# Attention stage of a fused layer: local result from masked scores as weights, values streamed

## The reference, cut to what matters

```python
def step(carry, xs):
    S, z = carry
    qc, kc, vcc = xs
    scores = jnp.einsum('bhid,bhjd->bhij', qc, kc) * mask
    num = jnp.einsum('bhij,bhje->bhie', scores, vcc) + jnp.einsum('bhid,bhde->bhie', qc, S)
    den = scores.sum(-1) + jnp.einsum('bhid,bhd->bhi', qc, z)
    out = num / jnp.clip(den, EPS)[..., None]
    S = S + jnp.einsum('bhjd,bhje->bhde', kc, vcc)
    z = z + kc.sum(2)
    return ((S, z), out)
```

```python
gprob = jax.nn.sigmoid(jax.nn.relu(coarse_repr @ eg_w1.T + eg_b1) @ eg_w2.T + eg_b2)
...
output = gate * memory_output + (1.0 - gate) * local_output
output = output.transpose(0, 2, 1, 3).reshape(B, S, H)
return output @ w_o.T
```

## Time and profile before

| what | us |
|---|---|
| median of 3 runs (679.31 to 690.9) | 687.66 |
| profiled execution | 685.47 |
| its span, first to last instruction | 683.6 |
| TensorE products busy | 601.4 |
| VectorE busy | 490.6 |
| ScalarE busy | 342.1 |
| GpSimd busy | 287.2 |

### The profile page before, as it was taken

One profiled execution on the slowest core, in us unless ns is written; L12 is line 12 of the kernel. 1 busy time (PEld: TensorE's weight loads), 2 busy tenths in 40 slices (PEclk: granted clock), 3 DMA queues, 4 the chain that ended last, 5 costly groups with the idle time before them and its releaser, 6 DMA issues. The chain is left out here.

```text
span 683.6 us, 23842 instructions
## 1 busy us (share of the span) xinstructions
PE 601.4 (88%) x8665; PEld 500.9 (73%) x8665; DVE 490.6 (72%) x1461; ACT 342.1 (50%) x870; POOL 287.2 (42%) x375
## 2 busy tenths in 40 slices
PE   1999998998995999999999588988989899889995
PEld 0787786887875899999999476766766676667773
DVE  3484565465575677777777566888888888878896
ACT  4538548548544444444444334555555555555542
POOL 2055064074072830000000303567666766666664
PEclk9999999999998899999999756999999999999997
DMA  9025535446156344445554502432443244323120
GB/s 306 34 106 200 198 138 204 164 152 217 74 199 234 113 129 154 152 150 152 156 164 128 156 23 67 131 95 66 144 142 95 66 157 130 95 66 95 34 66 32
DMA packets 62230, 88.60 MB, mean 130 GB/s; under 512 B 8532, under 2 KB 48436, under 8 KB 62132
## 3 DMA queue, kind: packets, MB, share of 16 engines
q1 hardware_dynamic: 52340, 66.61, 29.3%
q0 software_dynamic: 7520, 20.07, 9.3%
q10 hardware_dynamic: 2272, 0.53, 0.4%
HBM read 46.94 MB, written 40.24 MB: 128 GB/s over the span
## 5 line engine op out<-in xcount | busy, mean ns | idle before, releaser
L1703 POOL DMA_INDIRECT yg<-d_grouped_y,from_row x64 | 63.7, 996 | 15.5 <-issue 11.6
L986 ACT ACTIVATE silu<-e_up 128x176 f32<-128x176 f32 x72 | 22.9, 318 | 91.0 <-PE e_up L91 91.0
L89 PE MATMUL e_up<-wb,xb 128*128 x144 | 51.0, 354 | 1.5 <-DVE xb L1009 1.5
L1639 DVE TENSOR_TENSOR probs<-a_ring,causal_s 128x256 f32<-128x256 f32 x128 | 45.2, 414 | 9.3 <-PE a_ring L1400 8.9
L1545 ACT ACTIVATE hid<-a_ring,b 64x128 f32<-64x128 f32 x32 | 11.6, 363 | 79.0 <-PE a_ring L1428 75.8
L1528 ACT ACTIVATE with_mem<-a_ring 128x340 f32<-128x340 f32 x128 | 46.8, 447 | 4.5 <-PE a_ring L1381 4.5
L91 PE MATMUL e_up<-wb,xb 128*128 x144 | 46.9, 326 | 0.0
L90 PE MATMUL e_up<-wb,xb 128*128 x144 | 46.8, 325 | 0.0
L833 POOL TENSOR_TENSOR ticks<-lane 128x1 f32<-128x1 f32 x4 | 2.2, 561 | 97.7 <-DVE slot_i L746 97.7
L1418 PE MATMUL a_ring<-wo,attT 128*128 128x256 f32 x128 | 37.3, 416 | 6.5 <-ACT attT L1537 3.2
L1023 DVE TENSOR_TENSOR h_sb<-e_up,silu 128x128 f32<-128x128 f32 x72 | 21.0, 292 | 29.8 <-ACT silu L986 23.0
(11 more groups left out here) (290 smaller groups left out, 2064.6 us busy)
## 6 DMA issues: line engine op xcount, KB each, us to landing
v<-d_rows SPq DMA_DIRECT2D x77, 128.0 KB, 2.0
d_grouped_y<-y_sb SPq DMA_DIRECT2D x73, 128.0 KB, 1.9
d_v<-v_half SPq DMA_DIRECT2D x8, 544.0 KB
d_q<-halves SPq DMA_DIRECT2D x8, 512.0 KB
d_k<-halves SPq DMA_DIRECT2D x8, 512.0 KB
total<-d_base SPq DMA_DIRECT2D x8, 512.0 KB
out<-total SPq DMA_DIRECT2D x7, 512.0 KB, 3.9
v<-d_v SPq DMA_DIRECT2D x6, 544.0 KB
```

Source lines behind the costliest of these rows:

```text
L89: pe.matmul(out, a[0], b[0], start=start, stop=False)
L1639: dve.tensor_tensor(probs[:, j, :, :], ps[:, 0:4 * CH].rearrange("p (h i) -> p h i", i=CH), causal[:, :].unsqueeze(1).broadcast_to([P, 4, ...
L1703: pool.indirect_dma_start(yg[tile % GATHERS][:, k, :], None, d["grouped_y"], bass.IndirectOffsetOnAxis(ap=c["from"][:, k, tile:tile + 1], ...
```

## The change

The `values` step goes, and with it its two banks, ScalarE's two copies and the buffer `valT`. In `local` the masked scores `probs` (64 x 64 for a head and half) become the weights and the 17 columns of `v` stream; the result comes out with tokens on the partitions, in the bank and place where the state products already are, and is added to them. Half 0 uses partitions 0 to 63 of both memories, half 1 uses 64 to 127. The ring has 15 uses a tile, and the bank of `local` now follows that of `oproj` by seven. In the list, `state` with j = 1 moves in front of `gate`. VectorE's masking waits for `local` of the tile before, where it waited for its `values`.

```diff
-        order += [("values", b, t, 0), ("values", b, t, 1), ("gate", b, t, 0)]
         if t < NT - 1:
             order.append(("state", b, t, 1))
+        order.append(("gate", b, t, 0))
...
-                    elif what == "values":
-
-                        to = [ps, use_bank(pe, (what, b, n, 1))]
-                        for n_done, g in enumerate((0, 2, 1, 3)):
-                            if n_done % 2 == 0:
-                                since(pe, s_probs, b * NT * 4 + t * 4 + n_done + 2)
-                            for h in range(2):
-                                of = slice(h * CH, (h + 1) * CH)
-                                for i in range(4):
-                                    m, pair, r = g // 2, 2 * (g % 2) + i // 2, i % 2
-                                    mm = pe.matmul(to[h][VC * i:VC * i + HE, g * CH:(g + 1) * CH], v_of[of, b % 2, t, 4 * g + i, :],
-                                                   probs[of, pair, 2 * m + r, :], start=True, stop=True)
-                                if g == 3:
-                                    mm.then_inc(ready["values"], 1)
-                        continue
...
-                        since(pe, s_valT, b * 2 * NT + 2 * (t + 1))
-                        for g in range(4):
-                            mm = pe.matmul(ps[:, g * P:(g + 1) * P], valT[:, g, :], c["ident"][:, :],
-                                           start=(t == 0 and g == 0), stop=True, is_transpose=True,
-                                           skip_group_check=(t > 0 or g > 0))
+                        since(pe, s_probs, b * NT * 4 + t * 4 + 4)
+                        for n_done in range(NH):
+                            m, pair, r = n_done // HH, n_done % HH // 2, n_done % 2
+                            for h in range(2):
+                                of = slice(h * CH, (h + 1) * CH)
+                                mm = pe.matmul(ps[of, n_done * VC:n_done * VC + HE], probs[of, pair, 2 * m + r, :],
+                                               v_of[of, b % 2, t, n_done, :],
+                                               start=(t == 0 and n_done == 0), stop=True,
+                                               skip_group_check=(t > 0 or n_done > 0))
...
-                    elif what == "values":
-                        since(act, ready["local"], b * NT + t)
-                        act.activation(valT[:, :, j * CH:(j + 1) * CH], ps[:, 0:4 * CH].rearrange("p (g n) -> p g n", g=4),
-                                       ACT.Copy).then_inc(s_valT, 1)
...
-                        since(dve, ready["values"], b * 2 * NT + 2 * t)
+                        since(dve, ready["local"], b * NT + t)
```

More of the change, by code:

```diff
@@ L1190, in attention_phase @@
         ones = c["before"]
-        valT = sb("valT", [P, 4, P])
         with_mem = [sb(f"with_mem{q}", [P, NP, WN + NR2]) for q in range(3)]
@@ L1252, in attention_phase @@
                  ("mean", "norms", "keys", "scores", "outT", "coarseT",
-                  "hidden", "values", "local", "gate", "state", "oproj")}
-        s_valT = sem("a_valT")
+                  "hidden", "local", "gate", "state", "oproj")}
         s_mask = sem("a_mask")
@@ L1267, in attention_phase @@
             "mean": 1, "norms": NB3 * NT, "keys": NT, "scores": 4 * NT, "outT": NT, "coarseT": NT, "hidden": NT,
-            "values": 2 * NT, "local": NT, "gate": NT, "state": STATES, "oproj": NT}
+            "local": NT, "gate": NT, "state": STATES, "oproj": NT}
         last_reader = {
@@ L1272, in attention_phase @@
             "keys": s_ktok, "scores": s_probs, "outT": s_attT, "coarseT": s_coarseT, "hidden": s_hid,
-            "values": s_valT, "local": s_local, "gate": s_e, "oproj": s_sum}
+            "local": s_local, "gate": s_e, "oproj": s_sum}
         def nth(name, n, j):
-            return {"scores": 4 * n + j, "norms": NB3 * n + j, "values": 2 * n + j}.get(name, n) + 1
+            return {"scores": 4 * n + j, "norms": NB3 * n + j}.get(name, n) + 1
         def read_count(b, name, n, j):
@@ L1361, in walk @@
                     tok = slice(t * P, (t + 1) * P)
-                    if what in ("scores", "norms", "values") and j:
+                    if what in ("scores", "norms") and j:
                         continue
@@ L1507, in walk @@
                         continue
-                    if what not in ("keys", "outT", "coarseT", "hidden", "values", "gate",
+                    if what not in ("keys", "outT", "coarseT", "hidden", "gate",
                                     "mexp", "norms", "rows"):
```

## The result

The changed kernel takes 702.7 us as the median of four runs (698.87 to 709.37). The kernel before, run beside it, takes 684.6 (679.31 to 690.9). The ratio is 1.0253, with an interval from 1.0188 to 1.0318: slower, most likely by over 2%. The ratio is of the fast executions alone; 709.37 was a slow one. Forecast was 685, with no change.

The account below looks back on a forecast made before the run. A loop over GpSimd's sum and gathers was taken to bind each attention tile. From 685.47 us profiled, -3 and +1.5 gave 684.0, or 686.2 with the median's offset; 685 was forecast, 8 in 10 for 670 to 708.

Parts of the forecast that it names:

- likeliest case: Attention stage: the loop over GpSimd still binds, so time stays within 678 to 694 us; chance 0.62.
- Steady cost: 0: Attention tiles at full clock: scores start 0.25 us late, VectorE's later waits take it up, so nothing is lost.
- The cover: VectorE's waits of 0.46 to 0.97 us a tile absorb late scores, until new products exceed about 2.2 to 2.7 us.
- at full clock but for the first 20 us: TensorE's clock in the attention stage, about 404 to 672 us, as read from the profile before the change.
- The price of the new products: TensorE's 64 local products a tile: 1.73 us, with two quadrants loading at once, 54 ns each load.
- the slow rival: All 64 weight loads of the local products go one after another, 3.46 us a tile, about 720 us; chance 0.14.
- The loop over GpSimd: Sum and gathers 6.33 us, 0.48 to the fold, fold and products 1.64, 0.08 onward: 8.53 us sets the tile.
- The first two tiles: Attention's start at about half clock: new products 3.46 us against 2.76 removed, 0.7 a tile, +1.5 us for both.
- The rows' wait: GpSimd waits 5.5 us in 14 tiles for ScalarE's scaled rows behind the copies; 3 us counted as gain.
- The moved state update: Second state update ahead of gate waits for the first fold; local results still arrive in time, so cost 0.
- rival for faster: TensorE and ScalarE bind the attention tile, so stops and the rows' wait go: 17 us, about 669; chance 0.17.

Follow-up runs that it names:

- e1_stream64: Changed kernel with each new local product streaming 64 columns of values instead of 17, same loads: 685.5 us, ratio 1.0016 to the kernel before.
- e6_keep_clock: Changed kernel with 32 columns streamed and one extra 256-column product a tile before each second state update: 704.2 us, median of four.

## Why the prediction was wrong

The forecast was no change; measured was a loss of 18 us, inside the range (up to 708) and outside the likeliest case's own (678 to 694). The step that failed is "Steady cost: 0. The cover ends when the new products take over about 2.2 to 2.7 us", and under it the premise "at full clock but for the first 20 us", read from the earlier trace rows and carried over to the changed kernel without a word.

- *The clock, left out.* It was counted for the first two tiles alone. But the change takes away the 64 streams of 64 columns that line 1440 had, and puts loads of 64 columns with streams of 17 in their place. After that the granted clock falls again and again. Shown by e1_stream64: the same loads in the same order with 64 columns streamed, and clock and time are back. The 16.1 us between the two profiled executions (700.6 and 684.5) go with the clock: 53 us more at 1.2 GHz after 424, and 16 more before (0.39 x 20 / 0.5), so 0.23 us of time for each us at the lower clock. The two parts differ: 6.5 of the 16.1 us are there at the first output projection (424.7 against 418.3), 0.4 for each us, and 9.6 come after it, 0.18 for each. A path that ran through TensorE alone would lose half a us for each. That it is less after 424 fits the slack of the loop, which pays a part.
- *The price of the new products.* Estimated 1.73 us by loads at 54 ns for a pair of quadrants, measured 1.97, so 62 ns a pair. The two quadrants do load at once (two loads one after the other would be 108), and the slow rival (3.46) is out. The Trainium skill ("TensorE: Matmul & The Clock Gate", Part 3), by which a load overlaps a running product only in other row groups, gave 2.2; the measurement lies between the two. With 64 columns streamed, and the prediction's 0.84 ns a column for the stream too, an estimate by that rule is 54 + 54 a pair, 3.46 us, where that run has its scores 2.01 us after its first local product; there the trace does not agree.
- *The loop over GpSimd.* Right as the limit of the kernel before, and of the changed one as long as the clock is up: e1_stream64 shows the loop as nearly its whole chain in the attention stage, the two runs with plain loads show the gathers as the cause of the late signal. But the loop binds by little: without the gathers the kernel before gains 1.2% (0.4 to 2.0), and its tiles at full clock go from 8.43 to 8.22 us, not to 7.5.
- *How deep the cover is.* The prediction read it from VectorE's waits (0.46 to 0.97 us). TensorE's own length of a tile, 7.89 us at full clock, against the 8.53 of the loop leaves 0.64, which fits the chain of e6_keep_clock. At full clock the forecast's step holds, then: 1.97 us is under its 2.2 to 2.7. A fall of the clock for 3.4 us costs TensorE 1.25 us and more: it goes through the cover in the tile in which it comes.
- *The first two tiles.* Counted 1.5 us. The output projection of the first tile starts 2.4 us later (424.7 against 422.3). With 64 columns it starts at 418.3: the clock rises earlier there than in either kernel.
- *The rows' wait.* Right as a wait (5.5 to 0.7 us), and worth nothing.
- *The moved state update.* Costed at 0, measured 0 in both directions.

That the loop over TensorE and ScalarE binds (669) was a rival for faster. TensorE did come to bind, but with a longer path.

Why e1_stream64 takes 8.41 us a tile (first to last start of the output projection, 418.3 to 678.9, over 31) and the kernel before 8.28 (422.3 to 678.9) was not followed further. The 4 us are made up for by the earlier rise of the clock; so a few us of the loss may be longer tiles and not the clock, which the scatter of single tiles leaves open. Nor is it shown what else than the width of the streams could hold the clock: the one attempt settled nothing. Why streams of 17 columns behind loads of 64 lose the clock, no run shows.

## What to carry to other kernels

A change that cuts the columns streamed and keeps or adds weight loads makes TensorE's clock a term of the sum: ask of every stretch not only how long the engine is busy but what it is busy with, and give the fall of the clock a chance and a price of its own. Before such a cover is called enough, work out the length of TensorE's own path in a tile and halve the speed of a part of it. When busy time rises on an engine whose work was cut, look at the clock first, over several executions and not one; here one kernel with the same loads and wider streams settled it.

## What the runs showed of the hardware

- TensorE's clock fell from 2.4 to 1.2 GHz in stretches before which the engine was busy most of the time (9.85 of 10.90 us), with 2 us of each tile in loads of 64 columns and streams of 17. With plain loads it was busy for 9.87 of the 10 us ahead of the fall at 543.07. The falls of the kernel before with the move came behind less: 8.4, 8.1 and 7.0 of 10 us. The Trainium skill ("TensorE: Matmul & The Clock Gate", Part 1, "HAM oscillation — how this bites in real kernels") puts such falls down to the gaps in which TensorE waits. For the changed kernel the trace does not agree: its longest gap between 424 and 690 is 0.76 us, the kernel before has one of 1.67 (496.7) and no fall near it, and the falls go away with wider streams alone.
- A stream of 64 columns costs next to nothing more than one of 17 when the load has 64. The timeline of the kernel with 64 columns streamed, its local products and the scores behind them:

```profile
568.95 2.08 PE L1450 MATMUL a_ring<-v,probs 64*64 64x64 f32 x64
570.96 1.03 PE L1398 MATMUL a_ring<-sqT,masked 32*64 32x64 f32 x64
```

  The start of the scores lies 2.01 us after the start of the local products; with 17 columns it is 1.97 (571.56 to 573.53 in the changed kernel's timeline). So the stream does not set the pace there.
- Indirect gathers issued by GpSimd hold the signals of some of TensorE's small products: over 0.2 us late in 24 of 32 tiles of the kernel before with gathers, in none with plain loads of as many bytes.
